# A macaron block on one core: another order of the instructions in the attention core

## The reference, cut to what matters

```
x = x + 0.5 * ffn(layernorm(x))          # small attention of 4 heads, then a mixture of 8 experts
x = x + attn(layernorm(x))               # the part that the change touches lies in here
x = x + 0.5 * ffn(layernorm(x))

# attn, x is (8, 1024, 256), 16 heads of 16 columns
q, k, v = split(x @ W_attn.T + b_attn)
att = einsum('bhqd,bhkd->bhqk', q, k) / 4 + rel_bias     # rel_bias from the distance of key and query
att = softmax(where(causal, att, -inf))
y = einsum('bhqk,bhkd->bhqd', att, v) @ W_proj.T + b_proj
```

## Time and profile before

| | |
|---|---|
| median of three runs | 3017.53 us |
| the profiled execution, its own time | 3014.23 us |
| its span | 3012.5 us |
| TensorE, VectorE, ScalarE, GpSimd busy | 80%, 72%, 56%, 27% of the span |
| the attention core | about 1030 to 2209 us of the span |
| one round in it | about 34 us, 41 where the loop turns |

### The profile page before, as it was taken

One profiled execution on the slowest core, in us unless ns is written; L12 is line 12 of the kernel. 1 busy time (PEld: TensorE's weight loads), 2 busy tenths in 40 slices (PEclk: granted clock), 3 DMA queues, 4 the chain that ended last, 5 costly groups with the idle time before them and its releaser, 6 DMA issues. The chain is left out here.

```text
span 3012.5 us, 56962 instructions
## 1 busy us (share of the span) xinstructions
PE 2407.8 (80%) x15896; PEld 1442.6 (48%) x15896; DVE 2166.7 (72%) x5661; ACT 1687.0 (56%) x4003; POOL 827.5 (27%) x855
## 2 busy tenths in 40 slices
PE   3899998597399688888888888888876999996571
PEld 2566666575255233333333333333354666664450
DVE  3688887748588677777777777777634888886683
ACT  1455454337244278787787787787831554543471
POOL 0244343165444300000000000000012343442376
PEclk7899999899699789999999999999998999998796
DMA  6111111592255644343443333433234111111352
GB/s 189 43 64 54 51 63 35 175 319 84 75 168 170 149 83 83 89 84 82 91 86 80 82 82 80 81 82 80 41 105 153 50 64 42 63 56 47 107 163 88
DMA packets 232570, 284.92 MB, mean 95 GB/s; under 512 B 39904, under 2 KB 200736, under 8 KB 231664
## 3 DMA queue, kind: packets, MB, share of 16 engines
q1 hardware_dynamic: 206048, 221.95, 28.1%
q0 software_dynamic: 16384, 50.35, 5.2%
q10 hardware_dynamic: 9872, 9.45, 0.9%
HBM read 188.53 MB, written 93.11 MB: 93 GB/s over the span
## 5 line engine op out<-in xcount | busy, mean ns | idle before, releaser
L2047 DVE CUSTOM_DVE_ANT_0 banks<-banks,attn_bias 128x128 f32<-128x128 f32 (+7 forms) x1024 | 764.8, 774 | 241.4 <-PE banks L1904 209.9
L2007 ACT ACTIVATE attn_probT<-banks 128x512 f32<-128x512 f32 x1152 | 660.9, 602 | 248.4 <-PE banks L1921 237.4
L1904 PE MATMUL banks<-attn_kst,attn_qst 96*128 96x512 bf16 (+3 forms) x1536 | 428.7, 343 | 96.8 <-DVE attn_low L2047 54.9
L1921 PE MATMUL banks<-attn_qst,attn_kst 99*128 99x256 bf16 (+3 forms) x2176 | 429.9, 289 | 83.4 <-ACT banks L1995 58.1
L1921 PEld LDWEIGHTS banks<-attn_qst,attn_kst 99*128 99x128 bf16 x2176 | 180.4, 99 | 331.1 <-ACT banks L1995 154.7
L1943 PE MATMUL banks<-attn_probT,attn_vb 128*32 128x256 f32 (+3 forms) x4352 | 328.0, 413 | 4.8 <-ACT attn_oT L2019 0.6
L2105 POOL CAST attn_lowp<-attn_lowT 128x32 bf16<-128x32 f32 x64 | 13.4, 210 | 1038.4 <-DVE attn_lowT L2055 1038.4
L451 PE MATMUL banks<-ffn_a_xT,winT 128*128 128x512 f32 x512 | 251.0, 613 | 6.7 <-ACT ffn_a_kT L652 2.9
L1904 PEld LDWEIGHTS banks<-attn_kst,attn_qst 96*128 96x128 bf16 x1536 | 132.5, 100 | 245.5 <-DVE attn_low L2047 163.0
L1995 ACT COPY banks<-attn_biasT 128x512 f32<-128x512 f32 x384 | 234.4, 611 | 22.9 <-DMA attn_biasT<-neardT 22.9
L622 ACT ACTIVATE ffn_a_prob<-banks,ffn_a_negm 128x128 f32<-128x128 f32 x512 | 182.4, 379 | 13.1 <-DVE ffn_a_negm L760 11.5
(11 more groups left out here) (260 smaller groups left out, 4490.1 us busy)
## 6 DMA issues: line engine op xcount, KB each, us to landing
attn_qst<-qparts SPq DMA_DIRECT2D x384, 64.0 KB, 2.7
attn_kst<-kparts SPq DMA_DIRECT2D x192, 128.0 KB, 5.0
attn_biasT<-neardT SPq DMA_DIRECT2D x128, 192.0 KB, 5.7
rows<-ffn_a_xb SPq DMA_DIRECT2D x32, 512.0 KB, 2.9
rows<-ffn_a_y SPq DMA_DIRECT2D x32, 512.0 KB, 3.2
ffn_t_xs<-in_L_ffn_w_dram SPq DMA_DIRECT2D x16, 1024.0 KB, 11.5
attn_bias<-neard SPq DMA_DIRECT2D x128, 128.0 KB, 2.1
qparts<-qkv_part SPq DMA_DIRECT2D x32, 384.0 KB, 2.8
```

What stands on the lines that cost most here:

```text
L1904: mm = nc.tensor.matmul(score[k % 2][:, a:e], qst[0:K6, u, half, hh, ii * P:(ii + 1) * P], kst[0:K6, u, hh, a:e], start=True, stop=True)
L1921: mm = nc.tensor.matmul(tbank[t % 3][:, at:at + nb * P], kst[:, u, hh, j * P:(j + 1) * P], qst[:, u, half, hh, x:x + nb * P], start=(k == ...
L2007: nc.scalar.activation(probT[:, g % 2, i, 0:w], tbank[t % 3][:, 0:w], ACT.Exp, scale=-1.0).then_inc(s_exp, 1)
L2047: nc.vector.tensor_tensor_reduce(out=part, in0=part, in1=bias[:, hh, T - w:T], scale=1.0, scalar=BIG, op0=ALU.add, op1=ALU.min, accum_out= ...
```

## The change

The formula is gone. The order of a round is written out on TensorE and on ScalarE, instruction by instruction, and `SEQ` (the common order of steps and turnings, by which score buffers are taken) is written as: turning 0 ahead of step 30, turning 1 ahead of step 11. No instruction, buffer, semaphore or transfer is added or removed. The round's body on TensorE now begins with score step 0 and ends with weighting 8; on ScalarE it begins with the bias copy of tile 2 and ends with exponential 35.

```diff
-    def slot_cost(t):
-        return 1.1 if TILE[t][3] else 0.6
-
-    def step_cost(s):
-        half, _, ii = step(s)
-        return 0.29 + 0.133 * (half * HALF + ii + 1)
...
-    PV_AT = {FIRST[g + 1] + 1: g for g in range(NGR - 1)}
-    COPY_AT = [FIRST[HALF1] + 3, 3]
-    TURN_AT = [FIRST[HALF1] + 5, 5]
...
+    TURN_BEFORE = {30: 0, 11: 1}
+    SEQ = [x for s in range(STEPS + 1) for x in
+           ([("turn", TURN_BEFORE[s])] if s in TURN_BEFORE else []) + ([("step", s)] if s < STEPS else [])]
```

TensorE's body before and after, without the conditions for the first and last unit:

```diff
             def body(n, u):
-                for t in range(NT):
-                    tile(n, u, t)
-                    for k, (kind, x, at) in enumerate(SEQ):
-                        if at == t and kind == "step" and not last(n):
-                            free(n, k)
-                            scores(*after(n, u), x, k)
-                    if t in PV_AT:
-                        weigh_v(n, u, PV_AT[t])
-                    if t == 1 and not under(n, 1):
-                        weigh_v(*before(n, u), NGR - 1)
...
+                if nxt:
+                    scores(*after(n, u), 0, 0, n)
+                tile(n, u, 0)
...
+                if prev:
+                    turn_back(n - 1, 1, 11, n)
+                weigh_v(n, u, 1)
...
+                turn_back(n, 0, 31, n)
...
```

More of the change, by code:

```diff
@@ L1947, in weigh_v, with turn_back @@
                 mm.then_inc(s_PV, 1)
-            def turn_back(n, half, k):
+            def turn_back(n, half, k, now=None):
+                if now is not None:
+                    free(now, k)
                 pe.wait_ge(s_Osb, 2 * n + half + 1)
@@ L1964, in body @@
             def body(n, u):
-                for t in range(NT):
-                    tile(n, u, t)
-                    for k, (kind, x, at) in enumerate(SEQ):
-                        if at == t and kind == "step" and not last(n):
-                            free(n, k)
-                            scores(*after(n, u), x, k)
-                    if t in PV_AT:
-                        weigh_v(n, u, PV_AT[t])
-                    if t == 1 and not under(n, 1):
-                        weigh_v(*before(n, u), NGR - 1)
[L1975 to L1978, removed]
+                nxt, prev = not last(n), not under(n, 1)
@@ new lines, in body @@
+                tile(n, u, 11)
+                tile(n, u, 12)
+                if nxt:
+                    scores(*after(n, u), 15, 16, n)
+                tile(n, u, 13)
+                if nxt:
+                    scores(*after(n, u), 16, 17, n)
+                weigh_v(n, u, 2)
+                if nxt:
+                    scores(*after(n, u), 17, 18, n)
+                tile(n, u, 14)
+                if nxt:
+                    scores(*after(n, u), 18, 19, n)
+                tile(n, u, 15)
@@ new lines, in body @@
+                tile(n, u, 16)
+                if nxt:
+                    scores(*after(n, u), 19, 20, n)
+                weigh_v(n, u, 3)
+                if nxt:
+                    scores(*after(n, u), 20, 21, n)
+                tile(n, u, 17)
+                tile(n, u, 18)
+                if nxt:
+                    scores(*after(n, u), 21, 22, n)
+                tile(n, u, 19)
+                tile(n, u, 20)
+                if nxt:
+                    scores(*after(n, u), 22, 23, n)
@@ new lines, in body @@
+                tile(n, u, 21)
+                weigh_v(n, u, 4)
+                if nxt:
+                    scores(*after(n, u), 23, 24, n)
+                tile(n, u, 22)
+                tile(n, u, 23)
+                if nxt:
+                    scores(*after(n, u), 24, 25, n)
+                weigh_v(n, u, 5)
+                if nxt:
+                    scores(*after(n, u), 25, 26, n)
+                tile(n, u, 24)
+                tile(n, u, 25)
+                if nxt:
+                    scores(*after(n, u), 26, 27, n)
@@ L1979, in _ @@
+                tile(n, u, 33)
+                if nxt:
+                    scores(*after(n, u), 30, 32, n)
+                tile(n, u, 34)
+                weigh_v(n, u, 7)
+                if nxt:
+                    scores(*after(n, u), 31, 33, n)
+                tile(n, u, 35)
+                weigh_v(n, u, 8)
             triples(pe, NU, 3, 2, body)
@@ L2021, in body @@
             def body(n, u):
[L2022 to L2027, removed]
+                nxt, prev = not last(n), not under(n, 1)
+                seed(n, u, 2)
+                exps(n, u, 0)
+                seed(n, u, 3)
+                exps(n, u, 1)
+                exps(n, u, 2)
+                if prev:
+                    copy_o(n - 1, 1)
+                exps(n, u, 3)
+                exps(n, u, 4)
+                seed(n, u, 6)
+                seed(n, u, 7)
+                exps(n, u, 5)
+                exps(n, u, 6)
+                seed(n, u, 8)
+                seed(n, u, 9)
+                exps(n, u, 7)
+                exps(n, u, 8)
+                exps(n, u, 9)
+                exps(n, u, 10)
+                exps(n, u, 11)
+                exps(n, u, 12)
+                seed(n, u, 14)
+                exps(n, u, 13)
+                seed(n, u, 15)
+                seed(n, u, 16)
+                copy_o(n, 0)
+                exps(n, u, 14)
+                seed(n, u, 17)
+                exps(n, u, 15)
+                exps(n, u, 16)
+                exps(n, u, 17)
+                exps(n, u, 18)
+                exps(n, u, 19)
+                exps(n, u, 20)
+                seed(n, u, 22)
+                seed(n, u, 23)
+                exps(n, u, 21)
+                exps(n, u, 22)
+                seed(n, u, 24)
+                seed(n, u, 25)
+                exps(n, u, 23)
+                exps(n, u, 24)
+                exps(n, u, 25)
+                exps(n, u, 26)
+                exps(n, u, 27)
+                exps(n, u, 28)
+                exps(n, u, 29)
+                exps(n, u, 30)
+                exps(n, u, 31)
+                exps(n, u, 32)
+                exps(n, u, 33)
+                if nxt:
+                    seed(*after(n, u), 0)
+                exps(n, u, 34)
+                if nxt:
+                    seed(*after(n, u), 1)
+                exps(n, u, 35)
             act.wait_ge(s_marked, 3)
@@ L2078, in body @@
             def body(n, u):
[L2079 removed]
+                for k, (kind, x) in enumerate(SEQ):
                     if kind == "step" and not last(n):
```

72 lines of the change are left out of this document (57 added, 15 removed).

## The result

The changed kernel takes 2873.61 us (median of four, 2866.85 to 2877.51) against 3016.65 us for the kernel before in the same comparison. The ratio is 0.9529, with a 95% interval from 0.9508 to 0.955: 143 us gone. The forecast was 2901.5. The measured time lies outside the band from 2885 to 2930 that carried half of the chances, and 1.6 us inside the lower end of the range of 8 in 10, 2872 to 2962.

A forecast was written before the change was run, and what follows sets the result against it. No engine was full; nearly 7 of 34.4 us a round were order alone. Gains of 86.5 (normal), 25.6 (back-edge) and 3.9 us (edge round) made 116 off 3017.5: 2901.5 us, 8 in 10 range 2872 to 2962.

The forecast's parts named there:

- a period over a back edge: Round holding the loop's back edge, with stall and half clock: from 40.7 to 37.5 us, eight giving 25.6 us.
- The walk: New round laid out instruction by instruction, each starting at its engine's hand-over and the ends it awaits: 29.9 us.
- e34: ScalarE's exponential of key-major tile 34, claimed to wait for a weighting, with about 0.9 us of ScalarE idle.
- The self-waits: Five ScalarE bias copies directly behind the exponential whose bank they need wait for its end: 0.23 us each, 1.15 a round.
- e35: ScalarE's exponential of key-major tile 35, one of 36 exponentials a round, each taken at 0.49 us.
- the 0.3 that I added by choice: Allowance in a normal round for small gaps that no wait explains: 0.3 us, a hundredth of the round.
- The signs: Rounds near 30.2 us, eight near 37.5; TensorE's minimum and bias waits from about 99 us to under 40; turnings at stated times.
- The first: Rival: TensorE's busy time, 29.9, is nearer its floor; rounds of 31.9, 2955 us; chance 0.30 together with the second.
- second: Rival: ScalarE's self-waits cost 0.5 us each, 1.35 a round less gained, 2943 us; chance 0.30 together with the first.
- The third: Rival: the second row of minima arrives late and becomes the bound; rounds of 35.3 us, 3045 us; slower, chance 0.04.
- The fourth: Rival: the score products' position does nothing, since minima alone pace the round; within 0.2%, chance 0.02.
- The fifth: Rival: the walk with self-waits of 0.12 and no added 0.3; rounds of 29.3 us, 2872 us; below 2885, chance 0.14.

The follow-up runs named there:

- new_first: The kernel before, with the changed orders only in the first of each three rounds, right behind the loop's back edge: 2952.21 us, ratio 0.9794.
- new_rest: The changed kernel, with the old orders only in the first of each three rounds, right behind the loop's back edge: 2932.08 us, ratio 0.9736.
- before_twice: The kernel before, with score products of steps 0 to 11 issued twice in the round behind the back edge: 3093.0 us against 3087.92, ratio 1.0019.
- pe_new_act_old: The changed kernel with ScalarE's order as in the kernel before, TensorE and VectorE keeping the new order: 2919.37 us, ratio 0.9682.

## Why the prediction was right, and where not

Median 2873.6 against 2901.5 forecast, 143 gained against 116. The direction and the cause, order, were right, and so was the length of a normal period. The range was met by only 1.6 us, and the time lies where I had put 0.14, below 2885. Term by term, in the profiled spans (after's profiled execution is the fastest of its four; the core is taken from the first minimum to the last reciprocal):

| | forecast | measured |
|---|---|---|
| a normal period, 22 of them | 30.2, 86.5 us | 30.20, 86.5 us |
| a period over a back edge, 8 | 37.5, 25.6 us | 34.46, 50.1 us |
| one more round at the edges, and the last | 3.9 + 0 us | 8.2 us |
| the core | 116 us | 144.8 us |
| phases ahead and behind (unchanged) | 0 | 2.6 us (2.5 slower ahead, 5.1 faster behind) |

**The walk.** It held. In the round from 1214.41 on, V9 stands at 1.7 (1.6 forecast), V0 at 4.1 (4.1), T1 at 6.4 (6.2), t10 at 8.3 (8.4), V2 at 10.7 (10.5), V3 at 14.0 (13.8), T0 at 25.9 (25.6), V8 at 29.3 (28.8). V7 keeps e34 waiting, for 0.4 and 0.6 us in the two rounds read, where the walk had 0.9. But two of its terms were wrong and cancelled. The self-waits cost 0.14, not the 0.23 I took near the top of my bounds. ScalarE in after, b1, e35, b2, e0 and b3:

```profile
1213.34 0.59 ACT L2082 COPY banks<-attn_biasT 128x512 f32<-128x512 f32 x1
1213.87 0.59 ACT L2094 ACTIVATE attn_probT<-banks 128x512 f32<-128x512 f32 x1
1214.49 0.59 ACT L2082 COPY banks<-attn_biasT 128x512 f32<-128x512 f32 x1
1215.02 0.59 ACT L2094 ACTIVATE attn_probT<-banks 128x512 f32<-128x512 f32 x1
1215.64 0.59 ACT L2082 COPY banks<-attn_biasT 128x512 f32<-128x512 f32 x1
```

From an exponential to the copy that waits for it 0.62, against 0.48 without a wait. With 0.14 the walk gives 29.4, and the round without a loop is 29.33. And the 0.3 that I added by choice, for small gaps, stood where the loop costs 1.03 in each of its rounds. The average over the 22 came out at 30.20 because three of them are written out and take 29.3. So the walk is good to 0.1 us, and the exact 30.20 is luck.

**The back edge.** The term that was mis-sized, 37.5 against 34.46, 24.5 us of the 28.8 missing in the core. Its three parts, 3.37, 3.4 and 0.3, add up to 7.1 and not 7.3, which is 1.6 us of it. I took the stall at the longest of the eight; they are 2.6 to 3.4 us in both orders, 3.0 on average. And I took the half-clock stretch as fixed at 9.9 us and let denser work lose 3.4 in it. What is left for it is 34.46 - 30.36 - 3.0 = 1.1 us, because a denser start ends the stretch sooner: on average 4.7 us in after, where TensorE is busy all of the window shown, against 10.2 in before, where it is busy 8.31 of 9.90, or of the 8.94 from its restart on. new_first, new_rest and before_twice show it from three sides. The Trainium skill (TensorE: Matmul & The Clock Gate, What's actually happening) says that throttling is the default and activity releases it; I had weighed only that page's other side, that idle gaps bring it on.

**The last round.** I held it to be paced by ScalarE alone. It gained 4.3 us (8.2 less the 3.9 of one more round). The clock had a part: before, two stretches of it, 6.8 and 3.4 us, ran at half clock, and none of after's did. By stretch, before and after:

```profile
2175.00:2180.00 5.00, 3.92 (x33) 1.47 (x26) 0.00 (x0) 5.00 (x12) 0.00 (x0) 0.66 0.04 5
2180.00:2185.00 5.00, 4.46 (x34) 2.38 (x38) 0.68 (x2) 3.58 (x10) 0.00 (x0) 0.65 0.02 3
2195.00:2200.00 5.00, 4.20 (x36) 1.77 (x39) 0.00 (x0) 4.70 (x10) 0.00 (x0) 0.71 0.00 0
```

```profile
2035.00:2040.00 5.00, 3.77 (x48) 1.40 (x40) 0.89 (x3) 4.94 (x12) 0.91 (x4) 1.00 0.03 3
2040.00:2045.00 5.00, 4.05 (x39) 1.73 (x31) 0.68 (x2) 5.00 (x14) 0.00 (x0) 1.00 0.02 6
```

TensorE is no busier in after's rows, so why they kept the clock stays open.

**The parts.** Here the prediction was wrong though its sum was right. I gave the spread of the score products first place: alone it is worth nothing. I gave the weightings a short paragraph and no price: taken back, five of them cost 2.45 us a round, the most of all. T1's place is worth 1.0, and not for the narrow minimum that I named beside V0; ScalarE's order 1.4 (a normal period of 31.60 in pe_new_act_old against 30.20); T0's 0.25. The single losses add up to 5.1, more than the 3.9 gained: each part needs the others. That the score products taken back alone would cost something was not tested.

**The signs and the rivals.** TensorE's waits for minima and bias copies fell from 99 to 17 us, under the 40 named, and T1 and T0 stand where they were said to. The round over a back edge is not near 37.5. The first (31.9 a round) and second (self-waits of 0.5) fell with the period and with 0.14. The third did not come: the second row of minima is turned at 1214.66, its transfer issued at 1219.49, 4.83 us later as in the earlier trace rows, and t10 at 1222.7 has no wait ahead of it. The fourth was right in what it says of the score products' position and wrong in its result. The fifth gave 2872, nearly the measured time, but by a round of 29.3, which only the written-out rounds have.

## What to carry to other kernels

Where several in-order engines hand work round in a ring and none is full, place a long instruction where every engine that waits for its engine has work of its own, and feed those engines ahead of it. To find the places, look at where the idle time of a starved engine ends, and at what its releaser was doing until then. Test such an order by undoing one part at a time as well as by doing one alone: the score products looked like the cause by the waits, and were worth nothing alone. And look at what a loop costs apart from its order: here the written-out loop gave another 2.3%.

## What the runs showed of the hardware

A back edge of this loop stalls TensorE for 2.6 to 3.4 us, 3.0 on average, in both orders. The half clock behind it lasted 10.2 us in before, with TensorE busy 8.31 of 9.90 us, 6.7 us on average with 3840 further columns in the same order, and 3.4 or 6.8 us with the new order, in one case nothing. It was shorter where the clock fell later against TensorE's restart. Rounds inside the loop took 0.86 and 1.03 us longer than the same rounds written out, with about 265 more instructions each. A copy on ScalarE that waits for the exponential just ahead of it starts 0.62 us after that one's start, against 0.48 without the wait.
